# Two products on constants behind each pair of builds and behind the last of the sums, in the first layer of a two-layer graph network

## The reference, cut to what matters

```python
def reference(x, src, dst, edge_attr_32, L0_gnn_eps):      # x 12500 x 32, 400000 edges, dst sorted
    m = relu(x[src] + edge_attr_32)                        # layer 0
    neigh = segment_sum(m, dst, num_segments=12500)
    x = layernorm(x + (1.0 + eps[0]) * x + neigh)
    out_deg = clip(segment_sum(1, src), 1.0)               # layer 1
    in_deg = clip(segment_sum(1, dst), 1.0)
    h = x * rsqrt(out_deg)
    x = layernorm(x + segment_sum(h[src], dst) * rsqrt(in_deg))
    return x
```

## Time and profile before

| | |
|---|---|
| median of 3 runs | 6725.14 us (6714.55 to 6731.64) |
| the profiled execution | 6682.58 us, its span 6680.8 us |
| layer 0 | until about 5430 us of the span |
| layer 1 and the last norm | the rest |
| PE busy over the span | 53%, DVE 49%, ACT 41%, POOL 44% |

### The profile page before, as it was taken

One profiled execution on the slowest core, in us unless ns is written; L12 is line 12 of the kernel. 1 busy time (PEld: TensorE's weight loads), 2 busy tenths in 40 slices (PEclk: granted clock), 3 DMA queues, 4 the chain that ended last, 5 costly groups with the idle time before them and its releaser, 6 DMA issues. The chain is left out here.

```text
span 6680.8 us, 62572 instructions
## 1 busy us (share of the span) xinstructions
PE 3525.4 (53%) x21148; PEld 1678.9 (25%) x21148; DVE 3300.1 (49%) x4723; ACT 2725.0 (41%) x2907; POOL 2967.9 (44%) x3134
## 2 busy tenths in 40 slices
PE   1443444444444444444444444444444459999998
PEld 0111111111111111111111111111111128888887
DVE  3555545444444445555554544444444574444444
ACT  1433433333333333343333333333333345555554
POOL 6555555555555555555555555555555510000000
PEclk6665656565555655565555656555565569999999
DMA  2222222222222222222222222222222249999997
GB/s 57 92 92 92 92 92 92 92 92 85 81 87 92 90 77 92 92 92 92 92 92 92 92 92 92 80 85 87 92 88 79 93 153 328 325 326 327 326 327 254
DMA packets 269133, 867.70 MB, mean 130 GB/s; under 512 B 90218, under 2 KB 140218, under 8 KB 252602
## 3 DMA queue, kind: packets, MB, share of 16 engines
q1 hardware_dynamic: 169107, 815.98, 32.6%
q0 software_dynamic: 100000, 51.40, 5.1%
HBM read 486.77 MB, written 380.38 MB: 130 GB/s over the span
## 5 line engine op out<-in xcount | busy, mean ns | idle before, releaser
L166 POOL DMA_INDIRECT rows<-in_x,src_t x3125 | 2966.3, 949 | 2424.9 <-DMA dst_t<-in_dst 1491.0
L638 ACT ACTIVATE big<-built 128x980 bf16<-128x980 f32 x1500 | 1812.5, 1230 | 3108.7 <-remote 2365.9
L704 PE MATMUL built<-x_parts,b_hot 100*128 100x490 bf16 x3000 | 1357.5, 555 | 3046.3 <-ACT big L638 1575.9
L704 PEld LDWEIGHTS built<-x_parts,b_hot 100*128 100x128 bf16 x3000 | 223.7, 110 | 4052.2 <-issue 2094.3
L427 DVE TENSOR_TENSOR sum_ps<-sum_ps,rows 128x416 f32<-128x416 f32 x250 | 143.8, 575 | 2104.7 <-ACT sum_ps L616 2048.0
L684 PE MATMUL agg<-hot,msg 128*128 128x512 bf16 x3125 | 1016.9, 483 | 11.4 <-DVE msg L457 11.4
L1078 PE MATMUL applied<-counts,x_parts 128*96 128x160 bf16 x12250 | 916.2, 233 | 18.0 <-DVE x_parts L890 18.0
L1078 PEld LDWEIGHTS applied<-counts,x_parts 128*96 128x96 bf16 x12250 | 880.3, 123 | 79.3 <-issue 19.3
L146 DVE TENSOR_TENSOR x_parts<-iota_ps,hk_g 100x3920 bf16<-100x3920 f16 x375 | 820.3, 2188 | 0.0
L1034 ACT ACTIVATE counts<-built 128x980 bf16<-128x980 f32 x496 | 594.8, 1240 | 387.0 <-PE built L1061 387.0
L146 DVE TENSOR_TENSOR hot<-iota_ps,s_hi 128x5252 bf16<-128x5252 f16 x250 | 692.9, 2772 | 0.0
(11 more groups left out here) (132 smaller groups left out, 1420.9 us busy)
## 6 DMA issues: line engine op xcount, KB each, us to landing
stash<-big SPq DMA_DIRECT2D x125, 2940.0 KB, 8.5
counts<-stash SPq DMA_DIRECT2D x250, 1470.0 KB, 8.6
rows<-in_x,src_t POOLq DMA_INDIRECT x3125
edge_t<-in_edge_attr SPq DMA_DIRECT2D x61, 800.0 KB
big<-in_dst SPq DMA_DIRECT2D x1, 1562.5 KB
big<-in_src SPq DMA_DIRECT2D x1, 1562.5 KB
src_t<-in_src SPq DMA_DIRECT2D x61, 24.8 KB
dst_t<-in_dst SPq DMA_DIRECT2D x61, 24.8 KB
```

What stands on the lines that cost most here:

```text
L166: gp.indirect_dma_start(rows_d[:, j, :], None, nodes, bass.IndirectOffsetOnAxis(ap=src_d[:, j:j + 1].bitcast(U32), axis=0),).then_inc(s, 16)
L638: sc.activation(stage[:, slot % 2, q, :, d0:d0 + 2 * SPAN].rearrange("p c (b d) -> p b c d", b=2), built[n % 2][:, :, 0:KEYS].rearrange("p ...
L704: last = te.matmul(built[n % 2][:, b, 0:KEYS], b_hot[:, r, t, :], key_hot[:, r, t, :], start=True, stop=True)
```

## The change

Behind each pair of builds (twelve times in a step), and behind the last of the sums (once in a step), PE issues two more matmuls. They read the identity matrix, whose fp32 words are taken as bf16, so both operands are constants that lie in SBUF from the start. Each streams 256 columns against 64 columns of weights and writes to partitions 64 to 127 of the PSUM bank of the fold, where nobody reads. They wait for nothing and raise no semaphore. The increments `z_built[n]` and `z_agg` stay on the matmul ahead of them. That makes 26 more matmuls for each group, about 3,250 in all.

```diff
+                        spare = ident[:, :].bitcast(BF16)
+
+                        def idle_products(n):
+                            for _ in range(n):
+                                te.matmul(fold_bank[A1:P, 0:256], spare[:, 0:P - A1], spare[:, :], start=True, stop=True)
+
                         def step(g, slot, u):
...
                                     last = te.matmul(agg_bank[:, :], msg[:, j, :], hot[:, j, :], start=(j == 0), stop=(j == J - 1))
                                 if j1 == J:
                                     last.then_inc(z_agg, 1)
+                                    idle_products(2)
...
                                     last = te.matmul(built[n % 2][:, b, 0:KEYS], b_hot[:, r, t, :], key_hot[:, r, t, :], start=True, stop=True)
                                 last.then_inc(z_built[n], 1)
+                                idle_products(2)
                                 if n >= BP - 3:
 
                                     sum_up((n - BP + 3) * 3, (n - BP + 4) * 3)
```

## The result

The changed kernel takes 7397.69 us (median of 4 runs, 7391.55 to 7419.57), the kernel before beside it 6719.85 us (4 runs, 6713.83 to 6731.64): a ratio of 1.1012, 95% interval 1.0984 to 1.1041. The direction was forecast, the size was not: +678 us where +175 was expected, and a time above the range.

A forecast was written before the change was run, and what follows sets the result against it. The prediction took a chain to bound the kernel: POOL waiting for indices behind late steps in layer 0. 61 cycles at 2.8 us plus 4 us for the first run gave 175 us more, 6900 us, range 6705 to 7130.

The forecast's parts named there:

- What bounds the kernel: Layer 0: a chain, not a busy engine; POOL waits 25 us per 87.4 us cycle for indices loaded after a late step.
- The price of a matmul in the crawl: Each matmul there costs 2.8 us, hardly depending on columns; a product of 256 columns was also taken at 2.8 us.
- the crawl: Stretch of each gather run in which matmuls end late; said to last from the clock's fall to about the gathers' end, 51 us.
- After the gathers' end: Pause behind each gather run: leftover pairs, products and sums take 11.3 to 14.8 us against 8.1, so 3.2 to 6.7 us more.
- What starts the crawl: In layer 0, a fall of TensorE's granted clock while gathers run was said to start the late matmul ends.
- all alike: ScalarE's 3032 us idle before evictions, over some 60 cycles, is 50 us each, so the cycles were taken as the same.
- The clock holds: Rival, 10 in 100, faster: products keep PE busy, no clock fall during gathers, gathers bound layer 0: about 5250 us.
- The fall comes later: Rival, 7 in 100, faster: clock falls 10 us later in each gather run, up to 8 us per cycle won: 6240 us.
- Hidden: Rival, 8 in 100, same: products cost 1.25 us or less a cycle, mostly covered: 6725 to 6800 us.
- Dear: Rival, 15 in 100, slower: fall as early or earlier, sums after the gathers at half clock, 6.7 us a cycle: 7134 us.

The follow-up runs named there:

- the run with the increments: Changed kernel with each added product replaced by a semaphore increment that nobody waits for, on chips without late matmul ends: 5163.01 us, ratio 0.9999; repeats 5163.55 to 5163.90 us.
- the wait: Kernel before, with GpSimd's gathers also waiting for the sums of three steps back, on the chip with late matmul ends: 5814.69 us, ratio 0.8692.

## Why the prediction was wrong

**What bounds the kernel** was read rightly: POOL's wait behind a late step. Its pauses took nearly all of the loss.

**The price of a matmul in the crawl**, 2.8 us whatever its columns, holds: 11.2 us for a pair and two products above, and 97% of the loss with products of 16 columns. The sign of the forecast rests on it.

**The step that failed is "After the gathers' end"**: "the last sum ends about 8.1 us after the gathers' end", taken as 8.1 us of work that the change's 11.3 to 14.8 us stand against. The crawl goes on for 8.0 to 8.3 us after a run of 50 gathers, and then the pending ends come at once. Before, almost nothing of the step was left at that moment: the last sums and pair 0 came out together at its end. So the 8.1 us were a delay of fixed length behind a run of 50 and not work that the added work could replace; they stay, and the work left over begins behind them. With the prediction's own bounds that is 11.3 to 14.8 us more in each cycle, in place of 3.2 to 6.7, and over 61 cycles 690 to 900 us. The pause grew by 11.7 us, and eviction 0 of the next step comes 20.5 - 8.1 = 12.4 us later, nearer the low end; the sums do run at full clock, 4.28 us (below). The earlier trace rows had it: pairs 11 and 0, with nineteen sums between them, were evicted 1.6 us apart, while nineteen sums take 4.27 us even at full clock. Sums that had really run after the gathers' end would have kept these two evictions further apart. Over the 60 cycles it is plainer: pair 11 is evicted anywhere from 1.2 us ahead of the gathers' end to 6.6 us behind it, and pair 0 always 8.0 to 8.2 us behind it. The nineteen sums had been issued long before:

```profile
3089.59 5.34 PE L684 MATMUL agg<-hot,msg 128*128 128x512 bf16 x19
```

**What starts the crawl** was read wrongly too. The granted clock of the cycle shown above (same columns as ahead):

```profile
2656.00:2665.50 9.50, 8.05 (x38) 2.91 (x36) 5.69 (x6) 3.99 (x5) 7.16 (x8) 1.00 0.71 284
2665.60:2715.00 49.40, 8.33 (x24) 1.67 (x24) 13.86 (x18) 7.16 (x8) 37.21 (x41) 0.50 0.11 22
```

and its timeline of PE, the issue of pairs 0 and 1:

```profile
2661.76 0.59 PE L711 MATMUL built<-x_parts,b_hot 100*128 100x490 bf16 x2
...
2662.62 0.59 PE L711 MATMUL built<-x_parts,b_hot 100*128 100x490 bf16 x2
```

Pair 0 should have ended by 2662.4, ScalarE was free, and the eviction is at 2663.68, still at 1.00. Pair 1 should have ended by 2663.2, ScalarE was free at 2665.3, and the eviction is at 2667.23. Both were issued, and the first evicted late, before the fall at 2665.5. The prediction named this sign: late pairs with no fall ahead mean that the reading is wrong. In the changed kernel pair 0 is evicted late ahead of the fall in all 60 cycles. Over all cycles the first late pair comes about 16 us after the gathers' start before and about 11 now, while the fall hardly moves (11.7 and 12.7 us).

The start of the trace before shows it as well. The copies of transposes, and the matmuls for the first two of them:

```profile
53.14 0.59 ACT L603 ACTIVATE hk_all<-built 100x500 f16<-100x500 f32 x1 [0.75 <-PE built L382]
54.58 0.59 ACT L603 ACTIVATE hk_all<-built 100x500 f16<-100x500 f32 x1 [0.85 <-PE built L382]
56.01 0.59 ACT L603 ACTIVATE hk_all<-built 100x500 f16<-100x500 f32 x1 [0.85 <-PE built L382]
51.67 1.40 PE L382 MATMUL built<-ident,big 125*100 125x125 f32 x8
```

ScalarE waits here for matmuls that were issued before it was free, with the clock at 1.00 until 57.2 us. In the run with the increments, on a chip without a crawl, the same copies follow each other without a gap:

```profile
48.67 8.45 ACT L603 ACTIVATE hk_all<-built 100x500 f16<-100x500 f32 x13
```

What is nearly the same in these places is the number of matmuls issued since the gathers' start: on average 36 to 37 before, 35 now and 35 with the narrow products, and 37 at the start of the trace, though the gathers had run for 43 us there. That the number starts the crawl is not shown. Before, it varies from 27 to 45, so the cycles are not "all alike" as the prediction has it; now it is nearly always the same pair of the program, and with runs of 25 gathers it is 28. For the sum this error nearly made up for another, which is luck: the crawl began some three pairs earlier than forecast and lasted 8 us longer, so that at its end pairs 9 to 11 and all sums were left in the cycle shown, where pairs 8 to 11 and all sums were forecast for the gathers' end.

Counted in the trace (means over the cycles), the result comes out so. A cycle has 102 matmuls before and 154 now, of which the trace has 152. From the gathers' start to 8.3 us past their end 80.3 of them are issued before and 71.1 now; left for the pause are 21.7 and 80.9, and the pause behind that moment takes 15.6 and 27.4 us. So 59 more matmuls cost 11.8 us, 0.20 us each on average. It is not the products' own time: on the crawl chip 80.1 matmuls are left with products of 256 columns and 80.9 with products of 16, and the pause behind that moment is 26.2 us with either. What costs there are the pairs and sums that have been pushed out of the crawl. That fewer are issued in the crawl though more stand there has its reason in what waits: the nineteen sums wait for no eviction, were all issued ahead and came out at once; a pair can't be issued before the eviction two pairs ahead. Timeline of PE behind the crawl, pair 9, the nineteen sums, and pair 0 of the next step:

```profile
2725.29 1.00 PE L711 MATMUL built<-x_parts,b_hot 100*128 100x490 bf16 x2 [4.76 <-ACT big L638]
...
2731.45 4.28 PE L690 MATMUL agg<-hot,msg 128*128 128x512 bf16 x19
...
2736.00 0.59 PE L711 MATMUL built<-x_parts,b_hot 100*128 100x490 bf16 x2
```

The sums take their 4.28 us here in full, behind the crawl.

**The rivals.** *The clock holds* did not occur, and couldn't have ended the crawl, since the fall doesn't start it; on the other five chips there is no crawl, and the time there is near the 5250 given for this rival, by the same bound of 31.3 us a group. *The fall comes later*: it came 1 us later and helped nothing. *Hidden*: refuted on the crawl chip; on four of the others products like these were hidden. *Dear* gave 7134 for sums at half clock; its 6.7 us a cycle lack the same 8.1 us.

The Trainium skill (TensorE: Matmul & The Clock Gate, Part 1) speaks of a clock stuck at a quarter. By columns, products of 16 would cost next to nothing at that clock; they cost 2.8 us each here, as much as those of 256, so a slow clock alone does not explain the crawl.

**Open.** What the crawl is. It was seen only while gathers ran and shortly after, and only on one of the six chips and where the result was measured. That a pair is issued on time and ends late, and that nineteen sums were issued within 5.3 us in the middle of a crawl, speaks for the ends and against instructions that come late, but the run that would show it (increments in the products' place) met the crawl in none of four tries. Whether the bytes that the gathers move or the number of gathers bring it wasn't tried on a crawl chip either, nor were the products together with the wait. Why the late ends go on for 4.1 us after a run of 25 gathers, 8.1 after one of 50 and 12.3 after one of 100 is not known.

## What to carry to other kernels

A delay that lies at the end of a stretch is either work or a fixed time, and the two answer differently to added work: see whether the things in it come one after the other or all at once. Where matmul ends come late while GpSimd gathers, count matmuls and not columns, and try shorter runs of gathers: here a wait that costs 4.9 us a group took 13% off. And measure on more than one chip: here the change costs 10% on one, and products like it cost about 0.1% at most on four others.

## What the hardware showed unexpectedly

One kernel takes 6690 us on one chip and 5163.5 to 5165.2 us on five others, with the same duration of a gather (0.95 us, 1.25 us from one to the next) and of an eviction (1.2 us) in the traces of both kinds. The difference is when matmuls end during gathers: after 28 to 37 of them on average, mostly one end each 2.8 us, from 1 to 512 columns alike, until 4.1, 8.1 or 12.3 us after a run of 25, 50 or 100 gathers. A fall of TensorE's granted clock does not start it: ends are late at 1.00 ahead of the fall on the one kind, and none is late at 0.50 on the other.
